# Expert-choice FFN: rows fetched and added back by indirect transfers instead of one-hot matrix products

## The chip, the cores and the metric

The kernel runs on one core of a Trainium2 chip. The metric is the device time of one execution in microseconds, lower is better. The core has TensorE (PE, matrix products; PEld is its weight load), VectorE (DVE), ScalarE (ACT), GpSimd (POOL) and SyncE (SP, which issues transfers here), and 16 DMA engines that all queues share. The queue name q0 stands for transfers that GpSimd issues, q1 for those of SyncE and ScalarE. SBUF is the on-chip memory of 128 partitions, PSUM the eight banks in which TensorE leaves results, DRAM the memory outside.

## The reference

Two transformer layers over x of 8 batches, 512 tokens and 128 channels, each with an attention and a mixture-of-experts FFN, with a modulation (scale, shift, gate per batch) around each. The change is in the FFN of the first layer, cut here to what it computes:

```python
# x: (n=8, t=512, d=128) modulated norm of the tokens; e = 8 experts; k = 2*512/8 = 128
scores = jnp.einsum('ntd,ed->nte', x, gate_w)
probs = jax.nn.softmax(scores, axis=-1)
g, m = jax.lax.top_k(probs.transpose(0, 2, 1), k)      # each expert chooses 128 tokens
xin = x[batch_idx, m]                                  # gather
h = jnp.einsum('nekd,edf->nekf', xin, w1)              # f = 512
h = jax.nn.gelu(h, approximate=False)
h = jnp.einsum('nekf,efd->nekd', h, w2)
out_tok = g[..., None] * h
out = jnp.zeros((n, t, d)).at[batch_idx, m].add(out_tok)   # scatter-add
```

The result, times the gate, is added to x; the second layer's attention reads that.

## The kernel before

The kernel is written engine by engine. One list of steps, made by `add(kind, ...)`, holds the order of the whole program; each engine walks the list and does its part of each step, waiting on semaphores. So what stands ahead in the list stands ahead in every engine's queue.

The stages, by the time at which they end in the profile: the attention of layer 0 (to 785 us) as 128 units of 5.8 us, 16 for each batch b; the FFN of layer 0 (785 to 1056 us); the attention of layer 1 as 192 units, 24 for each batch, with the second FFN's routing among them; the second FFN. In a unit of the first attention, `project` steps for the next batch make queries and keys: PE's product, ACT's copy to `raw`, two POOL products (`rope_a` L2278, `rope_b` L2280), a DVE shuffle (L1923) and a POOL sum (L2291 or L2294). `late` is one POOL product of each unit (L2330). The router's probabilities of a batch go to `prob_tok`.

The FFN works on halves of four batches and on experts x; a step r (0 to 15) is half r // 8, expert r % 8, with 4 x 128 chosen rows at once.

- **Selection** (`select`), for each half on 32 partitions (4 batches x 8 experts): 16 times the eight largest of 512 (MAX8, L1984) and their removal (MATCH_REPLACE8, L1987), then threshold, ties, running counts and slot numbers (L1989 to L2015). Half 0 is selected within the attention, half 1 during steps 0 to 5.
- **Gather**: DVE compares slot numbers with an iota into bf16 one-hot matrices (`onehots`, L2028), ACT and POOL split the tokens into three bf16 parts (`token_parts`), and PE multiplies both, 24 products of 512 columns and 32 small ones for each batch (`gather`). The gates are gathered likewise (`split_prob`).
- **Up and down**: `up0` (4 products of 512 columns, fp32), GELU on ACT, `down0` (16 products of 128 columns), and DVE's multiplication by the gate (L2045) into `y_whole`.
- **Return**: ACT and POOL split each result into three bf16 parts (`y_split`), for each batch and expert PE spreads slot numbers (`slots`, 64 products), DVE compares them (L2067), and PE adds three products into the batch's bank (`back`); DVE adds it to `xT` (L2073, semaphore `x1_ready`). `back` of batch 0 stands between the halves, that of batches 1 to 7 behind step 15 (997 to 1056 us).

During steps 8 to 15 batch 0 of the second attention is prepared: `tokens`, `stat` (two POOL instructions), `center`, `norm`, `project` of key and query, `qk_parts` (four POOL instructions each) and `copies` (four, L2304). Then SP, in this order, writes the parts (`parts_out`), the four query copies (`copy_out`), loads them (`qload`, 8), loads late tables (L1103 to L1107, after the last `down0`) and loads `q_st` and `k_st` by 12 `stack` transfers into 8 partitions each (L1132), the query's six behind `back` of half 0. The first unit of the second attention waits for them. `q_zero` is a POOL memset of `prob`.

## Time and profile before

| what | us |
| --- | --- |
| median of 3 runs | 1920.51 |
| lowest, highest | 1912.13, 1920.54 |
| span of the profiled execution | 1921.2 |
| TensorE busy in it | 1731.9 (90%) |
| VectorE, GpSimd, ScalarE busy | 1151.9, 784.0, 708.0 |
| first attention / first FFN / rest | 785.4 / 270.4 / 865.4 |

The page of the profile gives busy time by engine, the span in 40 slices, the transfers, the chain of work that ended last and the costliest groups of instructions. Its TensorE is busy in nearly every slice, so the views that tell more are the stage table (busy time between two given times), the instructions in order of time of one engine with what ended the idle time before them, and the groups by line of a stretch. The 271 us of the first FFN hold all the work that the change replaces.

### The profile page before, as it was taken

Reading aid. Unit: us, or ns where it says so; the run is one execution under the profiler, and the core shown is the slowest. Engines: PE = TensorE matmul, PEld = TensorE weight load, DVE = VectorE, ACT = ScalarE, POOL = GpSimd, SP = SyncE. Lnnn points to the kernel's source line nnn. Section 1 sums busy time; section 2 is a strip of 40 time slices with the busy share of each in tenths; the row PEclk is TensorE's granted clock in tenths of the full one; section 3 lists DMA queues with packets and bytes.
Section 4 is the critical chain, followed back from the end, with each engine's and each line's share of the span. In section 5 each row is a group of like instructions: output and inputs, shape, how many; then the busy total and the mean of one; then the engine's idle time right before and its main releaser. Section 6 shows DMA issues by size and latency. Waiting matters only on the chain.

```text
span 1921.2 us, 76644 instructions
## 1 busy us (share of the span) xinstructions
PE 1731.9 (90%) x34928; PEld 1286.5 (67%) x34928; DVE 1151.9 (60%) x2281; ACT 708.0 (37%) x1073; POOL 784.0 (41%) x760
## 2 busy tenths in 40 slices
PE   6899999999999999798999989899899898878993
PEld 4667777777777767564562767677676676668883
DVE  4656666666787875667337655666666566544324
ACT  2333444344334333342430333343333343334341
POOL 2555646564646463324250403325232343015442
PEclk9999999999999999998999999999999999989997
DMA  9600000000000000300021123131321313025666
GB/s 306 203 2 2 2 2 2 2 2 2 2 2 2 2 2 2 111 1 1 1 67 19 40 61 77 40 87 46 84 73 43 85 44 84 20 66 179 205 205 185
DMA packets 81043, 113.48 MB, mean 59 GB/s; under 512 B 9485, under 2 KB 63505, under 8 KB 80288
## 3 DMA queue, kind: packets, MB, share of 16 engines
q1 hardware_dynamic: 71376, 97.16, 18.6%
q0 software_dynamic: 4544, 8.54, 1.3%
q8 instruction: 274, 4.49, 1.0%
q10 hardware_dynamic: 4800, 2.89, 0.6%
q14 instruction: 49, 0.40, 0.1%
HBM read 83.25 MB, written 45.68 MB: 67 GB/s over the span
## 4 chain that ended last, share of the span: by engine, by line
PE 66%; DVE 18%; issue 5%; ACT 4%; DMA 4%; POOL 2%; POOLq 0%; ACTq 0%; SPq 0%; DVEq 0%
PE psum L1189 63%; DVE colmax L1935 3%; DMA arena<-in_pack 3%; ACT prob L1664 3%; DVE colmax L2092 2%; DVE ctx_sum L1947 2%; DVE raw L1923 1%; DVE rowmax L1942 1%; PE psum L1544 1%; DVE arena L2028 1%; DVE rowmax L2100 1%; PE psum L1256 1%; ACT arena L1681 1%; PE psum L1264 1%; DVE prob L1987 1%
## 5 line engine op out<-in xcount | busy, mean ns | idle before, releaser
L1189 PE MATMUL psum<-arena 128*32 128x32 f32 (+8 forms) x10552 | 576.8, 247 | 43.9 <-issue 17.2
L1189 PEld LDWEIGHTS psum<-arena 128*32 128x32 f32 (+4 forms) x10552 | 453.5, 124 | 135.1 <-issue 61.0
L1681 ACT ACTIVATE arena<-psum 128x1024 f32<-128x1024 f32 (+1 forms) x192 | 169.4, 882 | 339.8 <-PE psum L1189 339.8
L1189 PE MATMUL psum<-neg_ident,rowmax 128*32 128x128 bf16 (+3 forms) x4352 | 208.2, 248 | 10.1 <-issue 8.4
L1935 DVE TENSOR_REDUCE colmax<-psum 128x512 bf16<-128x2048 f32 (+2 forms) x96 | 168.3, 1753 | 79.4 <-PE psum L1189 79.4
L2092 DVE TENSOR_REDUCE colmax<-psum 128x256 bf16<-128x768 f32 (+2 forms) x160 | 178.2, 1114 | 59.7 <-PE psum L1189 57.3
L1189 PE MATMUL psum<-prob,ffw 128*32 128x128 f32 x5120 | 201.5, 275 | 10.9 <-DVE rowmax L1942 9.6
L1696 ACT COPY ctx_sum<-psum 128x384 f32<-128x384 f32 x128 | 61.4, 479 | 378.4 <-PE psum L1189 330.8
L2330 POOL TENSOR_TENSOR arena<-ctx_sum 128x256 f32<-128x256 f32 x128 | 94.7, 740 | 228.5 <-DVE ctx_sum L1947 216.9
L2100 DVE TENSOR_REDUCE rowmax<-psum 128x2 bf16<-128x256 f32 (+1 forms) x192 | 97.9, 510 | 145.8 <-PE psum L1189 145.7
L1664 ACT ACTIVATE prob<-psum 128x2048 f32<-128x2048 f32 (+3 forms) x128 | 158.6, 1239 | 26.3 <-PE psum L1189 25.8
L1189 PEld LDWEIGHTS psum<-neg_ident,rowmax 128*32 128x32 bf16 (+1 forms) x4352 | 135.4, 97 | 45.9 <-issue 34.1
L1189 PEld LDWEIGHTS psum<-prob,ffw 128*32 128x32 f32 x5120 | 135.9, 110 | 39.9 <-DVE rowmax L1942 26.2
L2278 POOL TENSOR_TENSOR rope_a<-raw,arena 128x512 f32<-128x512 f32 x86 | 110.9, 1289 | 120.5 <-ACT raw L1644 111.3
L1947 DVE RECIPROCAL ctx_sum<-ctx_sum 128x128 f32<-128x128 f32 x128 | 120.3, 940 | 56.5 <-ACT ctx_sum L1696 56.3
L2384 POOL DMA_INDIRECT sent<-ffw x64 | 62.6, 978 | 218.3 <-DVE ffw L2207 171.4
L1189 PEld LDWEIGHTS psum<-ident_bf,colmax 128*128 128x128 bf16 x1024 | 74.5, 98 | 98.5 <-issue 32.4
L2280 POOL TENSOR_TENSOR rope_b<-raw,arena 128x512 f32<-128x512 f32 x96 | 126.3, 1316 | 33.9 <-ACT raw L1644 26.4
L1189 PE MATMUL psum<-ident_bf,colmax 128*128 128x128 bf16 x1024 | 111.0, 221 | 30.8 <-DVE colmax L2092 20.5
L1189 PE MATMUL psum<-hT,arena 128*128 128x512 f32 (+1 forms) x276 | 129.4, 560 | 4.3 <-ACT hT L1637 2.0
L1189 PE MATMUL psum<-prob,ones_col 128*32 128x128 f32 x2560 | 128.6, 273 | 0.0
L1189 PE MATMUL psum<-prob,arena 128*32 128x32 f32 (+2 forms) x6040 | 115.0, 210 | 10.3 <-DVE ctx_sum L2045 6.5
(270 smaller groups left out, 2532.1 us busy)
## 6 DMA issues: line engine op xcount, KB each, us to landing
arena<-in_pack SPq DMA_DIRECT2D x39, 578.0 KB, 3.9
sent<-in_empty SPq DMA_DIRECT2D x9, 2112.0 KB, 35.9
arena<-qk_parts SPq DMA_DIRECT2D x96, 128.0 KB
q_copies<-arena SPq DMA_DIRECT2D x32, 256.0 KB, 3.9
prob<-q_copies SPq DMA_DIRECT2D x128, 64.0 KB, 3.5
qk_parts<-arena SPq DMA_DIRECT2D x16, 384.0 KB, 3.7
arena<-sent SPq DMA_DIRECT2D x39, 132.0 KB, 3.3
ffw<-in_L_w SPq DMA_DIRECT2D x1, 2048.0 KB, 9.3
```

The costliest lines, as they stand in the source:

```text
L1189: return pe.matmul(o, lhsT, rhs, start=start, stop=stop, skip_group_check=True)
L1664: act.activation(prob_of(u).rearrange("p z j c -> p z (j c)"), scores_of(u).rearrange("p z j c -> p z (j c)"), ACT.Exp, scale=HD0 ** -0.5) ...
L1681: act.activation(probs_of(i)[:, :, h0 * P:(h0 + nh) * P], slot(n)[:, 0:(i + 1) * W].rearrange("p (j c) -> p j c", c=W), ACT.Exp, scale=HD1 ...
L1696: act.copy(ctx_sum[:, 0, n % 2, 0:CW], psum[:, CTX, 0:CW]).then_inc(ctx_drained, 1)
L1935: dve.tensor_reduce(colmax[:, n % 2, :].rearrange("p (z c) -> p z c", z=2), scores_of(u).rearrange("p z j c -> p z c j"), AX.X, ALU.max).t ...
L1947: dve.reciprocal(ctx_sum[:, 0, n % 2, 2 * P:CW], ctx_sum[:, 0, n % 2, 2 * P:CW]).then_inc(recip, 1)
L2092: dve.tensor_reduce(colmax[:, n % 2, 0:W], slot(n)[:, 0:(i + 1) * W].rearrange("p (j c) -> p c j", c=W), AX.X, ALU.max).then_inc(colmax1_d ...
L2100: dve.tensor_reduce(rowmax[:, n % 2, 0:nh], psum[:, MAX, 0:nh * P].rearrange("p (h k) -> p h k", k=P), AX.X, ALU.max).then_inc(max_done, 1)
L2278: chain.mark(pool.tensor_tensor(rope_a[:, z, :], raw[:, z, :], table[:, 0, :], ALU.mult))
L2280: chain.mark(pool.tensor_tensor(rope_b[:, z, :], raw[:, z, :], table[:, 1, :], ALU.mult))
L2330: chain.mark(pool.tensor_tensor(ctxT[b % 2][:, 2 * q:2 * q + 2, i * P:(i + 1) * P], ctx_sum[:, 0, n % 2, 0:2 * P].rearrange("p (c q) -> p ...
L2384: pool.indirect_dma_start(sent, bass.IndirectOffsetOnAxis(ap=dest[:, b % 2, h, n:n + 1], axis=0), sent_row[:, b % 2, h, n, :], None).then_ ...
```

## The change

The selection of an expert's 128 tokens now gives gates and token numbers themselves: each of the 16 rounds adds DVE's `max_index`, and threshold, counts and slots are gone. One pair of PE transposes brings both to `slot_gate` and `slot_token`. The centred tokens of each batch are also written to DRAM (`rows_out`, SP). `fetch` is one indirect transfer for each batch and expert, issued by POOL, 128 rows of 512 bytes into `fetched`; `rows_in` is four PE transposes and four ACT copies that apply scale and shift. After `down0` the gated result lies in one of four `y_buf`, and `send_back` adds it to DRAM (`added_rows`, zeroed at the start) by one indirect accumulating transfer for each batch, each waiting for the one before of the same batch. When all eight experts of a batch have landed, SP loads the sum (`acc_in`), PE transposes it and DVE adds it to `xT` (`x1`). The `x1` of batches 0 to 3 stand in steps 8 to 13, those of 4 to 7 in the second attention (units 21, 45, 69, 93). Weights are loaded expert by expert. The tables `onehots`, `token_parts`, `split_prob`, `y_split`, `slots` and `back` are gone on all engines.

```diff
-            return ([load] + [lambda r=r: add("sel_eight", half=half, r=r) for r in range(CAP // 8)] +
-                    [lambda k=k: add(k, half=half) for k in ("sel_threshold", "sel_equal", "sel_choice", "sel_slots",
-                                                               "sel_places")] +
...
+                for k in range(2 * E):
+                    late_side.setdefault(n + NU + 10 + k, []).append(
+                        lambda k=k: fetch(k // 2, range(k % 2 * 2, k % 2 * 2 + 2)))
...
+        between = {0: [center_f], 1: [router_f]}
+        behind = {0: [norm_f], 1: choose[0:3], 2: choose[3:7], 3: choose[7:11], 4: choose[11:15],
+                  5: choose[15:] + [lambda: fetch(E, range(HALF)), lambda: fetch(E + 1, range(HALF))],
+                  6: [lambda: fetch(E + 2, range(HALF))], 7: [lambda: fetch(E + 3, range(HALF))]}
+        for r in range(E):
+            if r + 1 < E:
+                up0(r + 1)
+            for f in between.get(r, ()):
+                f()
+            add("down0", r=r)
+            if r + 2 < E:
+                rows_in(r + 2)
+            add("send_back", r=r)
+            for f in behind.get(r, ()):
+                f()
+        rows_in(E)
+        rows_in(E + 1)
+        for b in range(ABUFS):
+            acc_in(b)
+        q_zero = q_cleared()
+        between = {E: [lambda: x1(0)], E + 1: [center_a], E + 2: [lambda: begin(key_a)], E + 3: [lambda: begin(query_a)],
+                   E + 4: [lambda: x1(2)], E + 5: [lambda: turn_band(1)]}
+        behind = {E: [tokens_a, stat_a, lambda: acc_in(ABUFS)], E + 1: [lambda: add("first_place"), norm_a],
+                  E + 2: [lambda: qk_parts("key", 0), lambda: x1(1)], E + 3: [lambda: copies(0)],
+                  E + 4: [lambda: qk_parts("query", 0), lambda: turn_band(0)], E + 5: [lambda: x1(3)],
+                  E + 6: [lambda: turn_band(2)]}
...
+            if r + 2 < 2 * E:
+                rows_in(r + 2)
+            if r + 4 < 2 * E:
+                fetch(r + 4, range(HALF))
+            add("send_back", r=r)
...
+        for b in range(HALF, B):
+            at(BATCH * (b - HALF) + 21, lambda b=b: x1(b))
...
+                    elif s.kind == "acc_in":
+                        b = s["b"]
+                        w.wait_ge(d_added[b], 16 * E)
...
+                        sp.dma_start(acc[:, b % ABUFS, :, :], added_rows[b // HALF][b % HALF * S:(b % HALF + 1) * S, :].rearrange(
...
                         if b < 2:
                             w.wait_ge(y_done, 2 * E)
-                            if what == "query":
-                                w.wait_ge(backed, HALF * E)
...
+                            chain.mark(dve.max(gates[:, eight], work))
+                            chain.wait()
+                            chain.mark(dve.max_index(token[:, eight], gates[:, eight], work))
...
+                    elif k == "fetch":
...
+                            pool.indirect_dma_start(
+                                fetched[:, x, q * D:(q + 1) * D], None, token_rows[hb],
+                                bass.IndirectOffsetOnAxis(ap=slot_token[:, row:row + 1], axis=0)).then_inc(
+                                    d_fetched[x], 16)
+                    elif k == "send_back":
...
+                        w.wait_ge(y_done, r + 1)
+                        for q in range(HALF):
+                            b = hb * HALF + q
+                            w.wait_ge(d_added[b], 16 * x)
+                            pool.indirect_dma_start(
+                                added_rows[hb], bass.IndirectOffsetOnAxis(ap=slot_token[:, b * E + x:b * E + x + 1], axis=0),
+                                y_buf[:, r % YBUFS, q * D:(q + 1) * D], None, compute_op=ALU.add).then_inc(d_added[b], 16)
```

GpSimd in the first attention, from the last units of batch 6 on. Before (L2278, L2280: the two products of a projection; L2294: its sum; L2330: `late`):

```order
L2330 TENSOR_TENSOR arena<-ctx_sum 128x2x128
L2278 TENSOR_TENSOR rope_a<-raw,arena 128x512
L2280 TENSOR_TENSOR rope_b<-raw,arena 128x512
L2294 TENSOR_TENSOR ffw<-rope_a,raw 128x512
L2330 TENSOR_TENSOR arena<-ctx_sum 128x2x128
```

The same place in the changed kernel (L2149, L2151, L2165 and L2201 are those lines there, L2214 is `fetch`):

```order
L2201 TENSOR_TENSOR arena<-ctx_sum 128x2x128
L2214 DMA arena<-token_rows0,slot_token 128x128 x2
L2149 TENSOR_TENSOR rope_a<-raw,arena 128x512
L2151 TENSOR_TENSOR rope_b<-raw,arena 128x512
L2165 TENSOR_TENSOR ffw<-rope_a,raw 128x512
L2201 TENSOR_TENSOR arena<-ctx_sum 128x2x128
L2214 DMA arena<-token_rows0,slot_token 128x128 x2
```

Two indirect transfers stand between each `late` and what comes next, in 16 units, 32 in all.

GpSimd from the end of the first half on, in the changed kernel (L2226 is `send_back`, L2237 `q_zero`, L2139 and L2141 `stat`):

```order
L2226 DMA added_rows0<-arena,slot_token 2048x128 x24
L2214 DMA arena<-token_rows1,slot_token 128x128 x8
L2226 DMA added_rows0<-arena,slot_token 2048x128 x4
L2214 DMA arena<-token_rows1,slot_token 128x128 x4
L2226 DMA added_rows0<-arena,slot_token 2048x128 x4
L2214 DMA arena<-token_rows1,slot_token 128x128 x4
L2237 MEMSET prob 128x4096
L2214 DMA arena<-token_rows1,slot_token 128x128 x4
L2226 DMA added_rows1<-arena,slot_token 2048x128 x4
L2139 TENSOR_SCALAR moments<-moments 128x4
L2141 TENSOR_TENSOR rstd<-moments,minus_half 128x4
```

The eight fetches ahead of step 6's results are those of steps 8 and 9; they wait for the selection, and `stat` of the next attention stands behind a fetch and a `send_back`.

TensorE from step 5 to step 8 in the changed kernel (L1439 `rows_in`, L1429 and L1430 the transposes of the selection, L1447 `x1`, L1230 `tokens`):

```order
L1439 MATMUL psum<-ident,arena 128x128 x4
L1429 MATMUL psum<-ident,prob 128x32
L1430 MATMUL psum<-ident,prob 128x32
L1163 MATMUL psum<-arena,ffw 128x512 x4
L1163 MATMUL psum<-ffw,arena 128x128 x32
L1439 MATMUL psum<-ident,arena 128x128 x8
L1163 MATMUL psum<-arena,ffw 128x512 x8
L1447 MATMUL psum<-ident,arena 128x128 x4
L1163 MATMUL psum<-ffw,arena 128x128 x16
L1439 MATMUL psum<-ident,arena 128x128 x4
L1230 MATMUL psum<-ident,xT 128x128 x4
```

The transposes of the selection stand ahead of `up0` of step 7 and `down0` of step 6, and `x1` of batch 0 ahead of `down0` of step 8.

## Rows read from the trace of the kernel before

**Rows 1.** Stage table: stretch, its length, busy us (count) by engine, clock, DMA share, GB/s

```profile
785.40:837.20 51.80, 43.05 (x324) 25.79 (x325) 32.46 (x47) 19.01 (x32) 15.55 (x14) 0.97 0.34 103
837.20:889.80 52.60, 51.20 (x313) 38.44 (x311) 47.38 (x73) 24.65 (x46) 25.43 (x21) 1.00 0.00 1
...
935.20:996.70 61.50, 60.52 (x341) 43.34 (x342) 10.05 (x18) 29.05 (x49) 33.70 (x31) 1.00 0.12 39
996.70:1055.80 59.10, 58.85 (x224) 16.95 (x223) 44.45 (x61) 2.52 (x3) 2.43 (x3) 1.00 0.19 30
```

**Rows 2.** Order of time, TensorE in the FFN: start, us, instructions [idle before, releaser]

```profile
797.29 2.02 PE L1189 MATMUL psum<-arena 128*128 128x128 f32 x16 [3.74 <-DVE xT L1952]
...
840.79 3.60 PE L1189 MATMUL psum<-arena,ffw 128*128 128x512 f32 x8
...
847.79 3.60 PE L1189 MATMUL psum<-arena,ffw 128*128 128x512 f32 x8
...
945.76 0.60 PE L1264 MATMUL psum<-ident,ctx_sum 128*128 128x128 f32 x4
```

**Rows 3.** Groups by line and form in the FFN: busy us, mean ns

```profile
L2361 POOL TENSOR_TENSOR ctx_sum<-ctx_sum,arena 128x512 f32<-128x512 f32 x16 | 20.0, 1250 | 45.6 <-ACT arena L1745 45.2
...
L1984 DVE MAX8 prob<-prob 32x8 f32<-32x512 f32 x16 | 10.9, 680 | 0.4
L1987 DVE MATCH_REPLACE8 prob<-prob 32x512 f32<-32x512 f32 x15 | 9.9, 663 | 0.0
...
L2008 DVE TENSOR_TENSOR_SCAN prob<-prob 32x512 f32<-32x512 f32 x1 | 2.1, 2066 | 0.0
```

**Rows 4.** Stage table in pieces of 4 us around a wait of TensorE (columns of rows 1)

```profile
896.00:900.00 4.00, 3.69 (x8) 0.76 (x8) 1.66 (x3) 1.24 (x2) 2.16 (x2) 0.50 0.00 0
...
908.00:912.00 4.00, 3.06 (x15) 1.20 (x13) 0.75 (x1) 0.00 (x0) 3.08 (x1) 0.98 0.01 4
```

**Rows 5.** Indirect transfers of the second FFN: two in order of time

```profile
1216.82 0.96 POOL L2384 DMA_INDIRECT sent<-ffw  x1 [0.30 <-issue]
1218.09 0.96 POOL L2384 DMA_INDIRECT sent<-ffw  x1 [0.30 <-issue]
```

**Rows 6.** View of tensor `sent`: durations of its issues; landing times

```profile
L2384 POOL DMA_INDIRECT sent<-ffw x64: 954/958/1232, 1215.3 to 1765.7; - x64
...
DMA to landing us min/median/max: 2.2/3.2/61.1
```

**Rows 7.** View of tensor `y_rows`: landing times of 78 indirect stores and 16 loads

```profile
DMA to landing us min/median/max: 2.1/3.3/10.4
```

**Rows 8.** Order of time, GpSimd in batch 6 of the first attention

```profile
676.40 0.72 POOL L2330 TENSOR_TENSOR arena<-ctx_sum 128x256 f32<-128x256 f32 x1
...
680.73 1.27 POOL L2294 TENSOR_TENSOR ffw<-rope_a,raw 128x512 f32<-128x512 f32 x1 [0.84 <-DVE raw L1923]
682.14 0.74 POOL L2330 TENSOR_TENSOR arena<-ctx_sum 128x256 f32<-128x256 f32 x1
```

**Rows 9.** Order of time, GpSimd in the FFN

```profile
888.49 2.01 POOL L2361 TENSOR_TENSOR ctx_sum<-ctx_sum,arena 128x512 f32<-128x512 f32 x1
...
908.92 3.51 POOL L2374 MEMSET prob<- 128x4096 f32 x1 [8.77 <-PE psum L1189]
...
971.98 4.39 POOL L2304 TENSOR_TENSOR arena<-rope_a,folds 128x512 f32<-128x512 f32 x4
```

**Rows 10.** Order of time, the transfers that SyncE issues at the end of the FFN

```profile
983.79 2.54 SPq L1113 DMA_DIRECT2D q_copies<-arena  x4
989.51 3.66 SPq L1143 DMA_DIRECT2D prob<-q_copies  x8
...
999.76 25.37 SPq L1132 DMA_DIRECT2D arena<-qk_parts  x12
```

**Rows 11.** Stage table, SyncE's: stretch, length, clock, DMA share, GB/s

```profile
1004.00:1006.00 2.00, 1.00 0.55 86
...
1010.00:1011.00 1.00, 1.00 0.13 27
```

More of the change, by code:

```diff
@@ L792, in turn_band, with q_cleared @@
             band_of[k] = add("band", aux=1, k=k)
-        ahead = {E: [norm_a, lambda: begin(key_a)], E + 1: [lambda: qk_parts("key", 0)],
-                 E + 2: [lambda: begin(query_a)], E + 3: [lambda: copies(0)],
-                 E + 4: [lambda: qk_parts("query", 0), lambda: turn_band(0)], E + 5: [lambda: turn_band(1)],
-                 E + 6: [lambda: turn_band(2)]}
-        add("up0", r=E)
+        def q_cleared():
+            return add("q_zero", pool=1)
+        out0()
+        rows_in(0)
@@ L799, in build @@
+        up0(E)
         for r in range(E, 2 * E):
             if r + 1 < 2 * E:
-                add("up0", r=r + 1)
-            else:
-                for k in range(BACKS // 2):
-                    add("slots", r=E + k)
+                up0(r + 1)
+            for f in between.get(r, ()):
+                f()
             add("down0", r=r)
-            if r > E:
-                split_y(r - 1)
-            for f in ahead.get(r, ()):
+            if r + 2 < 2 * E:
[3 more added lines that the diff above has]
+            add("send_back", r=r)
+            for f in behind.get(r, ()):
@@ L822, in build @@
             stack("key", 0, r)
[L823 to L825 removed]
         for r in range(len(PARTS_Q)):
             stack("query", 0, r)
+        for b in range(HALF, HALF + ABUFS):
+            acc_in(b)
         add("v_constants", pool=2)
```

483 lines of the change are left out of this document (152 added, 331 removed).

## The prediction

> **What bounds the kernel now.** First the stage table. TensorE is busy 51.2 of 52.6 us in steps 0 to 7, 60.5 of 61.5 in steps 8 to 15 and 58.9 of 59.1 in the last return; it idles mainly around the gathers (43.1 of 51.8 in the first) [rows 1]. So the FFN, 270.4 us, is bound by TensorE, and taking products away shortens it until another queue is late. TensorE's order of time gives the price of a step (`up0` and `down0`): from 840.79 to 847.79, 7.0 us [rows 2]. Last I read GpSimd's order of time, because the change gives this queue 128 indirect transfers: it issues one each 1.27 us (1216.82 to 1218.09) [rows 5]. Four, one step's worth in one direction, are 5.1 us. I place the new FFN on the clock of the old trace and add what happens elsewhere.
>
> **Attention of layer 0: +15 us.** The 32 fetches of half 0 stand behind `late` in 16 units, 2.5 us each. In units with a projection GpSimd has no room for that: `late` at 676.40, two products, the sum at 680.73 behind a wait of 0.84 for VectorE's shuffle, the next `late` at 682.14 [rows 8], a closed loop of 5.74 us beside a unit of 5.8. VectorE's shuffle waits in order for GpSimd's product, and the column maxima for which TensorE waits stand behind the shuffle, so the delay reaches TensorE. Ten projections lie in that stretch. About five inserts fall where nothing gives way, 12.6 us; I take 13. Nothing at all (their slack covers it) and ten full inserts, 25 us, are the bounds. `max_index` adds an instruction to each of 16 rounds. It is not in this trace; next to it stand MATCH_REPLACE8, 0.66 us, and as the costliest on that shape the scan, 2.07 [rows 3]. I take 0.75 with its load, since it too passes once over 512 elements. 12 us on VectorE, less about 8 for threshold and counts: +2.
>
> **FFN, start and steps 0 to 7.** Out-projections of batch 7 cost 2.0 each, and their wait of 3.7 for VectorE behind the one-hots goes [rows 2]; `up0` of step 0 can start at 797.0. Its weights, the first 0.5 MB of 4, have 11 us by then; the zeros and the tokens' copy in DRAM are written long before anyone reads them, and ScalarE, busy 24.7 of 52.6 us [rows 1], trades two casts a step for four small copies: 0 for each. Eight steps are 56.2, six `rows_in` of 0.45 (four transposes; the row of 0.60 holds the end of the last one) [rows 2] 2.7, norm, router and transposes 2.5, a wait for the norm 1.0. The selection decides more. A round is now 0.68 + 0.75 + 0.75, with gaps 2.2 us [rows 3], 35.5 for 16. It starts at 819.5, lets four gate multiplications (0.7 each) in, loses 2 us to order, and ends at 859.8. TensorE, whose transposes of it stand ahead of `up0` of step 7, is there at 848.9: a wait of 11.0, which the old selection, shorter by the indices, did not cause. Such a wait costs twice: TensorE's clock was 0.50 of full (1.2 GHz) in 896 to 900, after it had stood idle since 889.8, and 0.98 again in 908 to 912 [rows 4]; with half of the work at half speed I add 4. Half 0 ends at 874.4.
>
> **FFN, steps 8 to 15.** GpSimd can fetch half 1 from 861.5. Ahead of the last `send_back` of batch 0 it issues 17 transfers (8 fetches, 4 sends, 4 fetches, 1 send), 21.5 us, to 883.0. Landing 3.2 [rows 6], SP's issue 0.5 and the load about 3 give 889.7; TensorE has been there since 883 and waits 6.7 for `x1` of batch 0. Then `stat` stands behind two groups of four and the memset of 3.5 [rows 9], and the norm comes 6.2 late; the query's projection leaves its bank 4.7 late, because ACT's copy waits for `qk_parts` of the key. With 54 us of TensorE's own work from 893.7 step 15 ends at 958.6. GpSimd: from 883.0 three sends 3.8, four fetches 5.1, memset 3.5, then until the query's parts nine groups of four 45.5, `stat`, key and query work 13.2, `copies` 4.4 [rows 9], and the query's parts 3.7: 962.2. It is later than TensorE, so it sets the end.
>
> **The handover.** SP writes the parts (0.4), the copies 2.54, waits 3.2 for them, loads 3.66 [rows 10], tables 2.3: 974.4. Then 12 stacks stand in a row. Before, the first six were issued from 999.8 and the transfers had fallen to a share of 0.13 at 1010 to 1011 [rows 10, 11], 10 us; the other six hid under `back`. Both now lie open: 20.3. The second attention begins at 994.7, after some 36 us of an idle TensorE, instead of 1055.8. That is **-61.1**.
>
> With six in flight the share was 0.55 at 86 GB/s [rows 11]. The Trainium skill ("DMA: Bandwidth & Descriptors", "Why a DMA increments its semaphore by 16 and not by 1") has a transfer use as many engines as divide its outermost dimension, here 8 of 16, and the lowest ones; the trace agrees, and by it 12 take twice as long as 6. Without such a limit twelve at once could share the idle half and end 10 us earlier, at 1872 in all.
>
> **Attention of layer 1: +7 us.** Four `x1`, with 0.5 us of TensorE and 0.75 of VectorE each, some of it hidden: 3. The lower clock after the long wait: 4 [rows 4]. Everything later is unchanged. If the return's transfers of half 1 land late, nobody asks before unit 21.
>
> **Sum:** 1921.2 + 15 - 61.1 + 7 = **1882 us**. The profiled execution's span, 1921.2, and the median, 1920.5, are so near that I use the figure for both.
>
> **Rivals.**
> - *The fetches of half 0 hide, GpSimd is still late in the FFN.* For: VectorE loses the old threshold steps just there. Against: the loop of rows 8. 1882 - 15 = 1867.
> - *GpSimd is never late.* Then the query's parts, on which the end hangs, would be made at 941, TensorE's own pace, 21 us earlier. With the hidden fetches 1882 - 21 - 15 = 1846. Against: the count of transfers; it would need issues well under 1.27.
> - *Slower than before: accumulating transfers land late.* `send_back` of a step waits for the landing of the last step's for the same batch, and the whole GpSimd queue with it. No row shows one; plain indirect ones land after 3.2 and 3.3, the latest of `y_rows` after 10.4 [rows 6, 7]. I take 3.2 since all are 128 rows of a similar size. A step is 7.45 with its transposes, so up to about 6 us it costs nothing. At 13 half 0 takes 14.3 a step, 48 more on seven steps less the 15 around the selection, and half 1 adds 4.2 on five: +54, 1936. It passes the old time from about 12 on.
> - *Everything at its dear end*: ten full inserts (+12), the index at 1.4 (+10), GpSimd's chain late by 15 more: 1919, no change. That is also the case in which the removed products turn out to have been only a cover for the stacks.
> - *Contention at each issue.* GpSimd's product at 888.49 beside VectorE's one-hots took 2.01, where the mean of its line is 1.25 [rows 3, 9]. If each of some 60 transfers on the chain had those 0.76, and 15 in the attention: 1882 + 46 + 11 = 1939. Against it: 64 issues lie between 954 and 1232 ns [rows 6], with VectorE busy more than half of the time.
>
> The Trainium skill ("SBUF: State Buffer", box "The DVE blocks DMA trap (SWDGE)") says that VectorE in a two-port mode keeps GpSimd from writing descriptors. It would give the last rival; the narrow spread of the 64 issues speaks against it here.
>
> **How the numbers follow.** Forecast 0.52 (own range 1862 to 1906), hidden fetches 0.18, GpSimd never late 0.08, late landings 0.12, no change 0.05, contention 0.05. A measurement of this kernel can tell about 0.5%, 10 us, from no change. Faster by more than that, under 1911: 0.52 + 0.18 + 0.08 = 0.78. Within: the no-change case and an edge of the late landings, 0.07. Slower 0.15. The range from 1844 to 1914 takes in the first three and leaves out the slower ones.
>
> **What would show it.** In the changed kernel's profile: batch 6 and 7 of the first attention some 13 us longer, with VectorE's shuffle waiting for GpSimd; FIND_INDEX near 0.7 us; TensorE idle about 11 us before the selection's transposes and 7 before the first `x1`; accumulating transfers landing after 3 to 4 us; GpSimd past 60% busy from step 5 to 15; the first scores of the second attention some 209 us after the first attention's end, behind the last stack. I am wrong if the first attention keeps its length, if TensorE idles at `send_back`'s expense in half 0, or if the stacks land in under 15 us.

## The result and the profile after

The changed kernel takes 1906.3 us (median of 14 runs, 1893.9 to 1914.4), the kernel before 1918.9 in the same session: a ratio of 0.993, 95% interval 0.991 to 0.995. It is faster by 13 us, where 39 were forecast. The profiled execution's span is 1907.4 us.

The stage table of the changed kernel, with the columns of [rows 1]: half 0 up to step 3, steps 3 to 5, the selection and the first `x1`, steps 9 to 15, and the handover to the second attention.

```profile
811.50:849.10 37.60, 31.28 (x188) 24.39 (x188) 8.62 (x29) 17.86 (x37) 9.83 (x9) 0.95 0.56 153
849.10:877.10 28.00, 23.04 (x132) 16.69 (x133) 23.69 (x57) 12.93 (x25) 18.60 (x13) 1.00 0.32 29
877.10:935.20 58.10, 40.36 (x203) 28.60 (x203) 15.69 (x42) 18.23 (x37) 45.66 (x37) 0.88 0.35 57
935.20:1013.20 78.00, 54.61 (x308) 39.48 (x306) 11.45 (x23) 22.62 (x44) 65.22 (x53) 0.85 0.26 39
1013.20:1042.60 29.40, 0.00 (x0) 0.01 (x1) 0.69 (x1) 0.00 (x0) 20.74 (x13) 0.55 0.85 161
```

TensorE, busy almost throughout in [rows 1], is busy 149.3 of the 231.1 us, and GpSimd is the fullest engine from 877 on (110.9 of 136.1 up to 1013). TensorE's granted clock is 0.85 in the fourth row, where it waits often. The first attention now ends at 811.5 instead of 785.4, the FFN takes 231.1 instead of 270.4, and the rest 864.8 instead of 865.4: +26.1, -39.3 and -0.6, together -13.8, the difference of the two spans.

**First attention.** Two rows of each kernel, ScalarE's first and last exponential: in the kernel before 739.86 us lie between them, in the changed one 763.39, so 23.5 of the 26 arise inside. The other 2.5 lie ahead of the first exponential; kernels with the same start had it at 40.5 to 44.4, so they are not the change's.

```profile
41.26 1.88 ACT L1664 ACTIVATE prob<-psum 128x2048 f32<-128x2048 f32 x1 [7.46 <-PE psum L1189]
781.12 0.60 ACT L1664 ACTIVATE prob<-psum 128x512 f32<-128x512 f32 x1
```

```profile
43.75 1.88 ACT L1606 ACTIVATE prob<-psum 128x2048 f32<-128x2048 f32 x1 [9.04 <-PE psum L1163]
807.14 0.60 ACT L1606 ACTIVATE prob<-psum 128x512 f32<-128x512 f32 x1
```

GpSimd in order of time where a fetch pair meets a projection; it answers to [rows 8].

```profile
682.60 0.73 POOL L2201 TENSOR_TENSOR arena<-ctx_sum 128x256 f32<-128x256 f32 x1
683.48 0.99 POOL L2214 DMA_INDIRECT arena<-token_rows,slot_token  x1
684.77 0.94 POOL L2214 DMA_INDIRECT arena<-token_rows,slot_token  x1 [0.31 <-issue]
685.74 1.27 POOL L2149 TENSOR_TENSOR rope_a<-raw,arena 128x512 f32<-128x512 f32 x1
687.08 1.26 POOL L2151 TENSOR_TENSOR rope_b<-raw,arena 128x512 f32<-128x512 f32 x1
689.19 1.26 POOL L2165 TENSOR_TENSOR ffw<-rope_a,raw 128x512 f32<-128x512 f32 x1 [0.84 <-DVE raw L1841]
690.59 0.73 POOL L2201 TENSOR_TENSOR arena<-ctx_sum 128x256 f32<-128x256 f32 x1
```

The loop from one `late` to the next is 7.99 us instead of 5.74. The waits of VectorE in 672 to 811 show who pays (waiting instruction, releaser, us in total, times, longest):

```profile
DVE raw L1841 <- POOL rope_b L2151: 38.6, 9, 5.3
```

Before, this wait was 10.7 us, 6 times. The loops from one `late` to the next that hold a fetch pair, the same 16 in both traces, in us:

| loops with a fetch pair | count | before | changed | longer |
| --- | --- | --- | --- | --- |
| a projection's products behind the pair | 9 | 57.4 | 73.4 | 16.0 |
| no projection | 7 | 35.6 | 40.8 | 5.2 |

Five of the nine are 2.2 to 2.4 us longer, nearly all of a pair's 2.5; the other four, longer before (6.5 to 7.2 us), grow by 0.8 to 1.5. Together that is 21.2 of the 23.5 us; the rest was there ahead of the first pair.

**FFN.** The transfers by group (first row of the page, second of the stretch 811 to 1045) and the landing of the accumulating ones; they answer to [rows 5, 6].

```profile
L2226 POOL DMA_INDIRECT added_rows<-arena,slot_token x64 | 100.0, 1563 | 33.7 <-issue 16.8
...
L2214 POOL DMA_INDIRECT arena<-token_rows,slot_token x32 | 31.4, 982 | 10.1 <-issue 8.7 <-DVE raw L1841 1.0 <-DVE moments L1817 0.3
```

```profile
DMA to landing us min/median/max: 3.2/3.3/8.8
```

A fetch is a plain indirect transfer and costs what was forecast, 0.98 us and one each 1.27. An accumulating one takes 1.56 us, and with the 0.30 of issue between them one each 1.86.

TensorE's longest waits in the FFN, in order of time; they answer to [rows 2].

```profile
814.71 3.58 PE L1163 MATMUL psum<-arena 128*128 128x128 f32 x16 [3.36 <-POOLq L1021]
888.98 0.24 PE L1429 MATMUL psum<-ident,prob 32*128 32x32 f32 x1 [4.18 <-DVE prob L1910]
922.10 1.12 PE L1447 MATMUL psum<-ident,arena 128*128 128x128 f32 x4 [10.46 <-DMA arena<-added_rows]
946.30 1.12 PE L1238 MATMUL psum<-ident,ctx_sum 128*128 128x128 f32 x4 [7.83 <-DVE ctx_sum L1826]
980.07 6.24 PE L1163 MATMUL psum<-arena,ffw 128*128 128x512 f32 x8 [11.65 <-ACT arena L1657]
1042.62 0.59 PE L1163 MATMUL psum<-causal,ident_bf 128*128 128x512 bf16 x1 [29.46 <-DMA arena<-qk_parts]
```

A step of half 0, TensorE: `up0`, `down0`, `rows_in`, and again `up0`.

```profile
849.15 3.67 PE L1163 MATMUL psum<-arena,ffw 128*128 128x512 f32 x8 [1.21 <-issue]
852.65 3.73 PE L1163 MATMUL psum<-ffw,arena 128*128 128x128 f32 x32
856.23 0.60 PE L1439 MATMUL psum<-ident,arena 128*128 128x128 f32 x4
858.47 3.67 PE L1163 MATMUL psum<-arena,ffw 128*128 128x512 f32 x8 [1.64 <-issue]
```

It is 9.32 us, not 7.45: `up0` stands right behind its own transposes and waits for ScalarE's four copies of them. The profile calls that wait "issue"; the experiment with the rows ahead shows what it is.

The end of the query's parts on GpSimd, and SyncE's transfers after it, which answer to [rows 10]:

```profile
1010.23 1.16 POOL L2193 TENSOR_TENSOR arena<-ctx_sum,arena 128x512 bf16<-128x512 f32 x1
```

```profile
1011.79 2.52 SPq L1089 DMA_DIRECT2D q_copies<-arena  x4
1018.69 3.69 SPq L1117 DMA_DIRECT2D prob<-q_copies  x8
...
1025.25 6.91 SPq L1106 DMA_DIRECT2D arena<-qk_parts  x12
```

### The profile page after: what moved, and what is told of

Read it like the earlier page. It is cut to its first block, busy times and chain, and to the rows that moved or that the text cites. A ratio compares the mean times of both kernels' runs of the same rounds, so it can differ in the third digit from the quotient of the medians.

```text
span 1907.4 us, 75393 instructions
## 1 busy us (share of the span) xinstructions
PE 1648.4 (86%) x34316; PEld 1268.5 (67%) x34316; DVE 1054.0 (55%) x2219; ACT 695.3 (36%) x1071; POOL 880.8 (46%) x836
## 4 chain that ended last, share of the span: by engine, by line
PE 59%; DVE 16%; POOL 8%; issue 7%; DMA 5%; ACT 4%; SPq 1%; POOLq 0%; ACTq 0%; DVEq 0%
PE psum L1163 56%; DVE colmax L1853 3%; DMA arena<-in_pack 3%; POOL added_rows L2226 3%; ACT prob L1606 2%; DVE colmax L1963 2%; POOL arena L2214 2%; DVE ctx_sum L1865 2%; DVE raw L1841 1%; DVE rowmax L1860 1%; PE psum L1486 1%; POOL rope_a L2149 1%; POOL rope_b L2151 1%; DVE rowmax L1971 1%; PE psum L1238 1%
## 5 line engine op out<-in xcount | busy, mean ns | idle before, releaser
L1163 PEld LDWEIGHTS psum<-arena 128*32 128x32 f32 (+3 forms) x10296 | 448.5, 126 | 132.3 <-issue 59.2
L1163 PE MATMUL psum<-prob,ffw 128*32 128x128 f32 x5120 | 204.9, 278 | 23.5 <-DVE rowmax L1860 22.0
L1853 DVE TENSOR_REDUCE colmax<-psum 128x512 bf16<-128x2048 f32 (+2 forms) x96 | 168.4, 1754 | 77.5 <-PE psum L1163 77.5
L2201 POOL TENSOR_TENSOR arena<-ctx_sum 128x256 f32<-128x256 f32 x128 | 94.2, 736 | 221.6 <-DVE ctx_sum L1865 210.0
L1606 ACT ACTIVATE prob<-psum 128x2048 f32<-128x2048 f32 (+3 forms) x128 | 158.6, 1239 | 30.3 <-PE psum L1163 29.7
L2149 POOL TENSOR_TENSOR rope_a<-raw,arena 128x512 f32<-128x512 f32 x86 | 110.7, 1287 | 94.9 <-ACT raw L1586 86.6
L2151 POOL TENSOR_TENSOR rope_b<-raw,arena 128x512 f32<-128x512 f32 x96 | 125.4, 1307 | 36.6 <-ACT raw L1586 29.2
L1163 PE MATMUL psum<-causal,ident_bf 128*128 128x256 bf16 (+1 forms) x448 | 111.9, 297 | 35.1 <-DMA arena<-qk_parts 29.5
L2226 POOL DMA_INDIRECT added_rows<-arena,slot_token x64 | 100.0, 1563 | 33.7 <-issue 16.8
```

The source lines that it names most:

```text
L1163: return pe.matmul(o, lhsT, rhs, start=start, stop=stop, skip_group_check=True)
L1606: act.activation(prob_of(u).rearrange("p z j c -> p z (j c)"), scores_of(u).rearrange("p z j c -> p z (j c)"), ACT.Exp, scale=HD0 ** -0.5) ...
L1853: dve.tensor_reduce(colmax[:, n % 2, :].rearrange("p (z c) -> p z c", z=2), scores_of(u).rearrange("p z j c -> p z c j"), AX.X, ALU.max).t ...
L2149: chain.mark(pool.tensor_tensor(rope_a[:, z, :], raw[:, z, :], table[:, 0, :], ALU.mult))
L2151: chain.mark(pool.tensor_tensor(rope_b[:, z, :], raw[:, z, :], table[:, 1, :], ALU.mult))
L2201: chain.mark(pool.tensor_tensor(ctxT[b % 2][:, 2 * q:2 * q + 2, i * P:(i + 1) * P], ctx_sum[:, 0, n % 2, 0:2 * P].rearrange("p (c q) -> p ...
```

## The experiments

Each is the changed kernel with one or more edits. Two lengths are read from each trace. The **lag** is the time from ScalarE's first exponential to its last in the first attention, less 739.9, that of the kernel before. The **FFN stretch** goes from the first product of batch 7's output projection behind the barrier to the first scores of the second attention.

The first twelve runs were on three chips on which the kernel before takes 1988 to 1996 us. There the whole surplus lies in the second attention and what follows (the changed kernel: 944.8 us behind the first scores instead of 864.8, at a granted clock of 0.90 in 1300 to 1400 instead of 0.97), while both lengths above are the same within 2.2 us. The last three runs (e13 to e15) were on a chip on which the kernel before takes 1917.3, as on the first. So ratios are to the kernel before on the same chip, and the two lengths are compared directly. The changed kernel itself was not run on the chip of the last three.

| kernel | ratio, 95% interval | lag | FFN stretch |
| --- | --- | --- | --- |
| changed kernel (first chip) | 0.993 (0.991 to 0.995) | 23.5 | 227.9 |
| e5 changed kernel again | 0.995 (0.993 to 0.997) | 22.0 | 230.1 |
| e1 bursts of four | 0.997 (0.995 to 0.999) | 23.7 | 228.5 |
| e6 half 0 by SyncE, no choice | 0.981 (0.979 to 0.983) | 0.3 | 230.0 |
| e9 half 0 plain by GpSimd, no choice | 0.984 (0.981 to 0.987) | 5.6 | 230.1 |
| e7 pairs, two experts in the FFN | 0.988 (0.985 to 0.990) | 11.2 | 234.0 |
| e2 rows ahead | 0.995 (0.992 to 0.997) | 22.4 | 225.2 |
| e3 scatter without adding | 0.989 (0.985 to 0.992) | 22.0 | 214.3 |
| e4 parts first | 0.992 (0.989 to 0.995) | 22.0 | 220.8 |
| e8 pairs, rows, parts, tables | 0.989 (0.985 to 0.992) | 11.3 | 223.8 |
| e10 e8 without rows ahead | 0.989 (0.986 to 0.992) | 11.7 | 227.2 |
| e11 e8, selection's transposes later | 0.987 (0.984 to 0.991) | 11.7 | 225.5 |
| e12 e11 without parts first | 0.989 (0.987 to 0.992) | 11.7 | 234.6 |
| e13 fetches where GpSimd idles | 0.981 (0.977 to 0.984) | 3.0 | 232.0 |
| e14 e13 with rows, parts, tables | 0.980 (0.977 to 0.983) | 2.9 | 218.1 |
| e15 e14 without rows ahead | 0.983 (0.980 to 0.985) | 3.0 | 223.9 |

### What made the first attention longer

**e5**, the reference on such a chip: 

> The changed kernel unchanged, for a ratio taken on the chip of the experiments beside it: 0.993 of the kernel before, as on the first chip. If the second attention depends on the chip and not on the change, its length differs from 865 us by the same in every run of this chip.

Measured 0.995. What lies behind the first scores is 933 to 955 us long in all twelve runs of these chips, whatever the edit, so the surplus belongs to the chip, as written.

**e1**, half 0's fetches in eight bursts of four:

```diff
-                for k in range(2 * E):
-                    late_side.setdefault(n + NU + 10 + k, []).append(
-                        lambda k=k: fetch(k // 2, range(k % 2 * 2, k % 2 * 2 + 2)))
+                for k, at in enumerate((15, 20, 23, 24, 25, 26, 27, 28)):
+                    late_side.setdefault(n + NU + at, []).append(lambda k=k: fetch(k, range(HALF)))
```

> The changed kernel with one thing moved: the 32 fetches of half 0 stand in eight units of the first attention's last stretch without a projection (four batches at once, one expert each) instead of two at a time in 16 units in a row. Theory (inserts into GpSimd's loop with VectorE made the first attention longer by 21 us): the lag of batches 6 and 7 goes, the last context of attention 0 leaves 15 to 21 us earlier than the changed kernel's 811.5, nothing later changes, 1906 becomes 1886 to 1891. Rival (the added max_index and the selection on VectorE made it longer): the first attention keeps its length within 4 us and the time is 1902 to 1910. Rival 3 (eight bursts of 5 us each are as bad as 16 of 2.5): 1900 to 1910 with the lag now in batch 7 alone.

The theory's number failed and the third rival came true: until unit 120, with three bursts, the lag was 6.9 instead of 20.5, then it grew by 17 in the last seven units, with five. Four in a row, 5 us, nearly fill a unit of 5.8 by themselves.

**e6**, half 0's rows by SyncE:

```diff
+                    elif s.kind == "fetch" and s["r"] < E:
...
+                        for q in s["batches"]:
+                            sp.dma_start(fetched[:, x, q * D:(q + 1) * D], token_rows[0][q * S:q * S + P, :]).then_inc(
+                                d_direct, 16)
```

> The changed kernel, but half 0's rows come by 32 plain transfers that SyncE issues at the same places; it leaves out the choice in half 0 (the first 128 tokens of each batch are taken). max_index, the selection's waits, all landings and the sends stay. Theory (GpSimd's 32 issues made the first attention longer by 23 us, the index and the traffic almost nothing): the last context of attention 0 leaves 20 to 23 us earlier than the changed kernel's, all later lengths stay, 18 to 23 us under the changed kernel. Rival (max_index on VectorE, busy 70% there): 12 us or less of it goes. Rival (the rows' packets in the DMA engines hold up others): under 5 us goes.

The lag is 0.3, and the time (1954.6) 26 us under e5's 1981.1, 3 more than expected. So `max_index` costs the first attention nothing at its end (the lag is 2.8 at unit 106 and is made up again), plain transfers of the same size issued by SyncE cost nothing, and all of the lag goes with the indirect transfers on GpSimd's queue.

```profile
40.91 1.88 ACT L1614 ACTIVATE prob<-psum 128x2048 f32<-128x2048 f32 x1 [7.46 <-PE psum L1171]
781.05 0.60 ACT L1614 ACTIVATE prob<-psum 128x512 f32<-128x512 f32 x1
```

**e9**, the same plain transfers from GpSimd's queue:

```diff
+                        for q in s["batches"] if hb == 0 else ():
+                            pool.dma_start(fetched[:, x, q * D:(q + 1) * D], token_rows[0][q * S:q * S + P, :]).then_inc(
+                                d_fetched[x], 16)
```

> The changed kernel with half 0's 32 fetches as plain transfers, issued from GpSimd's queue at the same places; it leaves out the choice in half 0 (the first 128 tokens of each batch are taken). It tells what of the 22 us that the first attention lost is GpSimd's time and what is the kind of transfer. Theory (each transfer that GpSimd issues costs its queue about 1.25 us, whatever kind): the lag stays at 15 to 23 us. Rival (only an indirect one costs that, since each partition's index is read): issues under 0.5 us, lag under 5. In both cases: if TensorE's groups of products break up with idle time of kind 'issue' behind these too, the cause is how GpSimd's transfers are queued; if they do not, it is the indices.

Both numbers lie between theory and rival. From the view of `token_rows`, plain ahead of indirect:

```profile
L2213 POOL DMA_DIRECT2D arena<-token_rows x32: 544/577/793, 673.0 to 763.4; - x32
L2217 POOL DMA_INDIRECT arena<-token_rows,slot_token x32: 943/948/1404, 873.1 to 967.9; - x32
```

0.58 us with no gap behind it instead of 1.27, and a lag of 5.6 instead of 22. The lag follows GpSimd's time, not in proportion: 18 us of issuing made 5.6, 40 made 22 to 23.5. That the first part fits into slack is argued, not shown, since the kind of transfer changed too.

**e7**, 24 fetches in pairs in 12 units chosen as free of a projection, the last eight in the FFN:

```diff
+                for k, at in enumerate((12, 15, 16, 20, 23, 24, 25, 26, 27, 28, 29, 30)):
+                    late_side.setdefault(n + NU + at, []).append(
+                        lambda k=k: fetch(k // 2, range(k % 2 * 2, k % 2 * 2 + 2)))
...
+        behind = {0: [norm_f, lambda: fetch(E - 2, range(HALF))], 1: [lambda: fetch(E - 1, range(HALF))] + choose[0:3],
```

> The changed kernel with half 0's fetches in pairs in 12 of attention 0's units where GpSimd has no projection (24 of them), and the last eight behind steps 0 and 1 of the FFN. Theory of slack (GpSimd has 4.9 us of a 5.8 us unit free there, a pair takes 2.5, so nothing gives way): attention 0's lag falls from 23.5 to under 6 us, and the FFN stays within 2 us; 14 to 19 under the changed kernel. Rival (in the run with bursts of four the lag came in free units too, 3.3 us each, so a fetch holds up the others even where GpSimd has room): the lag stays at 12 or more, and the time within 8 us of the changed kernel.

Between the two cases: the lag is 11.2, and 13 us come off (1968.2). The FFN stretch is 3.9 longer than in e5, not within 2. Three of the 12 pairs stand directly ahead of a projection's products in GpSimd's queue after all, and these three loops are 6.3 us longer than in the kernel before. But half of the lag arises in units 120 to 127, where GpSimd itself waits 2.1 to 3.4 us in each unit. TensorE's groups break up there. In e7, while a pair's rows move:

```profile
761.06 0.59 PE L1163 MATMUL psum<-prob,ffw 128*32 128x128 f32 x6
761.93 0.44 PE L1163 MATMUL psum<-prob,ffw 128*32 128x128 f32 x6 [0.29 <-issue]
762.66 0.32 PE L1163 MATMUL psum<-prob,ffw 128*32 128x128 f32 x2 [0.29 <-issue]
```

From 672 to 783 us TensorE waits 2.9 us in this way ("issue") in e7 and 2.3 us in e5, but not at all in e9, whose plain transfers stand where e5 has its indirect ones. In the changed kernel's own trace and in e13 there is no such row either, and six of e13's pairs leave their loops as long as before, where e7's in the same six loops cost up to 1.4 us each. So it was seen with indirect transfers on the three slower chips only, and what connects the two is not settled here.

### What set the pace of the FFN

**e3**, the scatter without adding:

```diff
-                                y_buf[:, r % YBUFS, q * D:(q + 1) * D], None, compute_op=ALU.add).then_inc(d_added[b], 16)
+                                y_buf[:, r % YBUFS, q * D:(q + 1) * D], None).then_inc(d_added[b], 16)
```

> The changed kernel with the scatter plain instead of accumulating: it leaves out the adding, so that in a token's row the last expert's output stays. All 64 transfers, waits and landings stay. Theory (an accumulating transfer costs GpSimd 1.86 us an issue where a plain one costs 1.26, and GpSimd's queue sets x1 of batch 0 and the query's parts): 0.6 us less on each; about 8 stand ahead of the last send of batch 0 from the selection's end on, and 28 more until the query's parts: the second attention starts up to 17 us earlier, 1889 to 1896. Rival (TensorE's own steps set the end, GpSimd only looks late): under 4 us, 1902 to 1908. Second rival (accumulating and plain issue cost the same, the price is from the registers of this line): L2226 still shows about 1.56 us busy and 1.86 a period.

```profile
L2226 POOL DMA_INDIRECT added_rows<-arena,slot_token x64: 956/967/1108, 835.2 to 1008.8; - x64
```

The theory holds: 0.97 us instead of 1.56, and the FFN stretch is 15.8 shorter than in e5. The time goes just where the sends stand: from the selection's transposes to `x1` 29.7 us instead of 33.0, from `x1` to the query's parts 76.5 instead of 89.6, while the handover is 0.5 longer. In these two parts GpSimd issues 28 sends, and 28 times 0.59 us are 16.5. That is the price of "accumulating" on GpSimd's queue.

**e2**, the fetched rows' transposes ahead of `down0`:

```diff
-            add("down0", r=r)
             if r + 2 < E:
                 rows_in(r + 2)
+            add("down0", r=r)
```

> The changed kernel with the transposes of the fetched rows (rows_in of step r+2) put ahead of down0 of step r instead of behind it. Theory (up0 of the step after stands right behind its own rows and waits 1.65 us a step for ScalarE's four copies): the steps of half 0 fall from 9.3 to 7.6 us, seven of them, and half 1 gains 1.2 on up to six where GpSimd is not the bound: 12 to 19 us off, 1887 to 1894. Rival (the queue of GpSimd with its transfers sets the pace, TensorE's wait for copies is only where the slack shows): half 0 shortens, but the wait for the selection and for x1 of batch 0 grows by the same, 1900 to 1907.

The rival: steps fall to 7.44 us, as the rows show (`up0` to `up0`), and TensorE's wait for the selection grows from 4.2 to 9.6. Of some 13 us, about 5 reach the end (225.2 against 230.1, and nothing that the ratio shows). Five such steps stand ahead of the selection's transposes, 9.4 us: 5.4 of them go into the wait, and the selection itself ends 4.0 earlier.

```profile
849.34 3.60 PE L1163 MATMUL psum<-arena,ffw 128*128 128x512 f32 x8
852.77 0.60 PE L1439 MATMUL psum<-ident,arena 128*128 128x128 f32 x4
853.21 3.74 PE L1163 MATMUL psum<-ffw,arena 128*128 128x128 f32 x32
856.78 3.60 PE L1163 MATMUL psum<-arena,ffw 128*128 128x512 f32 x8
...
881.41 0.31 PE L1429 MATMUL psum<-ident,prob 32*128 32x32 f32 x1 [9.58 <-DVE prob L1910]
```

**e4**, GpSimd's other work of a step ahead of its transfers in steps 8 to 15:

```diff
...
+            for f in behind.get(r, ()):
+                f()
             if r + 4 < 2 * E:
                 fetch(r + 4, range(HALF))
             add("send_back", r=r)
-            for f in behind.get(r, ()):
-                f()
```

> The changed kernel with GpSimd's order inside steps 8 to 15 changed: tokens, statistics, norm, the memset, the parts of key and query and the copies stand ahead of that step's fetch and send_back instead of behind them. Theory (the second attention starts where the query's parts are made, and these stand behind transfers for which nobody waits yet): the parts come 7 to 20 us earlier, and 1906 becomes 1888 to 1899. Rival (x1 of batch 0 at 922 binds everything behind it, the transfers behind it only fill): 1902 to 1908. Rival on the other side (the sends come later, so that x1 of batches 1 and 2 and the fetches of steps 12 to 15 come late): TensorE idles in steps 12 to 15 and the time is 1910 or more.

The theory holds: the FFN stretch is 9.3 shorter than in e5. The query's parts are ready 190.0 us behind the stretch's start instead of 197.4, without a transfer less.

**e8**, all of these with e7's fetches, the table loads behind the stacks: 

> The changed kernel with the fetches of the run named before, the rows' transposes ahead of down0, GpSimd's parts ahead of its transfers in steps 8 to 15, and the five table loads behind the twelve stacks. If these are independent terms: attention 15, steps 3, parts 7, tables 2 to 3, about 27 us under the changed kernel, a ratio of 0.980 to the kernel before. If GpSimd's queue binds behind all of them, the terms don't add: 12 to 18 under it, 0.985.

1966.0 us, 15 under e5 on the same chip, and a ratio of 0.989: the second case, the terms do not add. Attention gave 11, but the FFN only 6 against e5, less than e4 alone. The selection's transposes come 1.9 earlier than in e5, but from there to `x1` it takes 36.4 us instead of 33.0.

**e10**, e8 without rows ahead: 

> The changed kernel with pairs of fetches in units without a projection, GpSimd's parts ahead of its transfers in steps 8 to 15, and the table loads behind the stacks; rows_in stands behind down0 as in the changed kernel. Theory (rows ahead of down0 only moves the wait to the selection, so leaving it out costs nothing): attention 11, FFN 7 to 11, together 18 to 22 under the changed kernel, ratio 0.984 to 0.986. Rival (the fetches of steps 6 and 7 behind steps 0 and 1 delay the sends until the selection ends): the FFN gains under 5.

Its rival: 227.2, 6 more than e4. Only 2.5 of these lie ahead of the selection's transposes, where the fetches behind steps 0 and 1 can delay the sends; 3.9 lie in the handover, and why is not shown.

**e11**, the selection's transposes behind `down0` of step 6:

```diff
+            if r == E - 2:
+                choose[17]()
+                fetch(E, range(HALF))
+                fetch(E + 1, range(HALF))
             add("send_back", r=r)
```

> The kernel with all four reorderings and one more: the selection's transposes stand behind down0 of step 6 on TensorE, ahead of that step's send_back on GpSimd, instead of behind step 5. Theory (TensorE, with the rows ahead of down0, reaches the selection 10.6 us early and could work a step meanwhile): that wait goes to 0 to 3, the step that it used to do afterwards is done, half 0 ends 7 to 10 us earlier; of that 3 to 8 reach the second attention, since fetch and send_back still stand in GpSimd's queue. Ratio 0.981 to 0.985. Rival (GpSimd's queue from the selection's end on sets everything): x1 of batch 0 is at the same time, 0.987 to 0.989 as with four reorderings.

TensorE's wait for the selection falls from 10.6 to 4.3, and then it waits 7.0 and 3.9 for the fetched rows; `x1` of batch 0 starts at 909.86 against 909.91 in e8. The rival holds: from the selection on, GpSimd's queue sets the time.

**e12**, e11 with the parts behind the transfers again: 

> As the run before, but with GpSimd's transfers ahead of its parts in steps 8 to 15, as in the changed kernel. Where the parts bind (as they did alone, 9 us of FFN): 7 to 10 us slower than the run before. Where x1 and the sends bind: within 3 us of it.

The stretch is 9.1 longer, as expected, but the medians differ by only 2.3 us, and the ratios (0.989 and 0.987) do not tell the two apart.

### Is it the transfers, or where they stand?

**e13**, only the fetches moved: 16 in pairs in eight units chosen as free of a projection, 12 right behind the barrier, four behind `stat`:

```diff
+                for k, at in enumerate((16, 20, 23, 24, 25, 26, 27, 28)):
+                    late_side.setdefault(n + NU + at, []).append(
+                        lambda k=k: fetch(k // 2, range(k % 2 * 2, k % 2 * 2 + 2)))
...
         out3()
+        for r in range(4, 7):
+            fetch(r, range(HALF))
         up0(0)
         tokens_f()
         stat_f()
+        fetch(7, range(HALF))
```

> The changed kernel with only the fetches of half 0 moved: those of experts 0 to 3 in eight pairs in units without a projection, those of 4 to 6 right behind the barrier, where GpSimd idles 16.1 us in the changed kernel (12 by 1.26 are 15.1), those of 7 behind the statistics of batch 7. Theory (the cost of a fetch is where it stands): attention 0's lag is 4 to 8 us instead of 22, the FFN within 2 us of 229, 13 to 18 under the changed kernel. Rival (fetches moved into the FFN delay it, as the two experts' behind steps 0 and 1 did by 4 to 6): FFN 233 or more, 8 to 12 under.

1884.4 us, a ratio of 0.981 where the changed kernel had 0.993: by the ratios some 20 us under it on this chip. The lag is 3.0, less than expected. Six of the eight pairs cost nothing (each of their loops is as long as in the kernel before, within 0.01 us); the other two stand directly ahead of a projection's products, and their loops are 1.8 and 2.2 us longer. GpSimd behind the barrier, first and last of 12 fetches and `stat`:

```profile
792.19 1.10 POOL L2217 DMA_INDIRECT arena<-token_rows,slot_token  x1 [0.16 <-issue]
...
806.12 0.94 POOL L2217 DMA_INDIRECT arena<-token_rows,slot_token  x1 [0.30 <-DVE moments L1820]
807.10 0.25 POOL L2142 TENSOR_SCALAR moments<-moments 128x4 f32<-128x4 f32 x1
```

So the queue had room for nearly all 32; the attention's 22 us were a matter of place. The FFN stretch is 2 to 4 longer, not within 2 of 229. It is the handover: TensorE's wait is 34.8 us instead of 29.5, since the twelve stacks take 22.8 instead of 17.4, although the query's parts come no later (195.5 us behind the stretch's start). Why was not traced.

**e14**, with e8's other three edits: 

> As the run before, with rows ahead of down0, GpSimd's parts ahead of its transfers in steps 8 to 15, and the table loads behind the stacks. Theory (terms add where each has idle time of its own): attention 14 to 18, FFN 216 to 219 instead of 229 (parts 9, rows 3): 25 to 30 under the changed kernel, ratio 0.979 to 0.982 to the kernel before. Rival (they meet in GpSimd's queue): FFN 222 or more, ratio 0.984 or more.

The FFN is 218.1, as the theory has it, and 13.9 under e13. The ratio is in the theory's range too, and by it the kernel is some 24 us under the changed one. But the total, 1880.8 (ratio 0.980), is only 3.6 under e13, within the intervals: what lies behind the first scores is 868.4 us instead of 862.0, of which 3.3 arise in its first 75 us, at a clock of 0.93 instead of 0.96. The rest was not traced further. Its ratio is the lowest of all, clear of the changed kernel's, but not told apart from e13's and e15's.

**e15**, e14 without rows ahead: 

> As the run before, but rows_in behind down0 as in the changed kernel. If the rows' place is worth 3 us here too: FFN 219 to 222 and 3 slower than the run before. If TensorE just waits longer for the selection: the same as the run before within 1.5.

223.9, 5.8 longer than e14 and more than expected: here the rows' place has a part of its own. 4.5 of it lie ahead of the selection's transposes, and from there to `x1` both take 33.2 us, unlike e8. In time it is 2.8 us, within the intervals.

## Why the prediction was right or wrong

The sign and the mechanism were right, the size was not: 13 to 14 us instead of 39. The measured 1906.3 lies at the upper edge of the forecast's own range (1862 to 1906) and inside the wide one (1844 to 1914). Two steps failed. The larger one is the price of a `send_back` on GpSimd's queue: the forecast took 1.27 us for every transfer, and an accumulating one measured 1.86. The other is the term for the inserts, 13 us, where the loops with a fetch pair became 21.2 us longer. Term by term:

- **Start and attention, +15 forecast, +26.1 measured.** 2.5 of it is the start. The mis-sized term is the 13 us for "about five inserts where nothing gives way". The loop of rows 8 was read rightly, and five projection loops did pay in full, 11.4 us. But the others were put at nothing: four projection loops paid 4.6 us in part, and the loops without a projection 5.2. (Nine projections meet a fetch pair, not ten.) The bound of ten full inserts, 25 us, was nearer the truth. TensorE's granted clock also fell, to 0.87 in 700 to 740, where it had been 1.00; but in e5 it was 1.00 from 672 to 803 and the lag still 22.0, so the clock hardly explains more than the 1.5 us between the two.
- **`max_index`, +2 forecast.** An instruction takes 0.67 us and its load 0.08, as forecast; in the attention it alone costs nothing (e6: lag 0.3). The 16 of half 1:

```profile
L1904 DVE FIND_INDEX8 prob<-prob 32x8 uint32<-32x512 f32 x16 | 10.8, 673 | 0.0
```

- **FFN to the selection's end, 74.4 us forecast, 77.5 measured** (from the attention's end). Two errors hid each other, which is luck. The step is 9.3 us and not 7.45, since ScalarE's copies had been taken to cost nothing, so TensorE arrives 9.8 us later than forecast; the wait for the selection is 4.2 and not 11. e2 shows how they are linked: 9.4 us less of steps lengthen the wait by 5.4 and move the selection's end by 4.0.
- **To `x1` of batch 0, 29.9 forecast, 33.1 measured** (888.98 to 922.10). The 12 fetches and 5 sends take 24.2 us and not 21.5: five sends at 1.86 are 3 more. The landing was 3.3, as assumed.
- **From `x1` to the query's parts, 72.5 forecast, 89.3 measured.** This is the largest error. The count was right: behind the last send of batch 0 (from 917.4 to 1011.4) GpSimd issues 23 sends and 20 fetches, the 43 that were counted. The price was not: I took 1.27, the period of plain indirect transfers [rows 5], for both kinds. 23 sends at 1.86 are 13.6 more. The trace had no accumulating transfer, and I bounded only when one lands, not what one costs to issue. The 28 sends of this part and the one before account for 16.5 of the 21.8 us by which the FFN was forecast too short, and e3, which takes only the adding away, gives 16.4 back in just these two parts.
- **Handover, 32.5 forecast, 31.2 measured.** The twelve stacks, 20.3 forecast, took 17.4 from the first issue to the first scores, and 17.1 to 25.0 in the other runs. The DMA share was 0.77 to 0.98 in three pieces of 2 us, with sends and sums of batches 4 to 6 among them, so this stretch bears out neither limit by itself. The forecast had followed the Trainium skill's rule on how many engines a transfer uses ("DMA: Bandwidth & Descriptors", "Why a DMA increments its semaphore by 16 and not by 1"); its 20.3 lies within the measured spread.
- **Second attention, +7 forecast, -0.6 measured.** Four `x1` and the lower clock after the handover leave no trace in its length. Whether something else gained what they cost, no run shows.
- **Rivals.** Late landings: refuted, 3.3 us median and 8.8 at most, and GpSimd waited 0.6 us in all for them. Contention at each issue: refuted, 64 fetches between 940 and 1405 ns with a median of 950, half of them beside a VectorE that is busy 49% of 700 to 740, the others beside one busy 15 to 27%. The Trainium skill warns of a trap ("SBUF: State Buffer", box "The DVE blocks DMA trap (SWDGE)"): while VectorE runs in a two-port mode, GpSimd cannot write descriptors. It does not show in these durations; whether VectorE ever ran in such a mode here, the trace does not say. Hidden fetches: refuted for this order, and almost true for another (e13).

From -61.1 to -39.3 in the FFN, and from +15 to +26.1 ahead of it, less the 7.6 that the second attention did not cost: 22 + 11 - 8 = 25 us, the distance from 1882 to 1907.

## What to carry to other kernels

An indirect transfer is work for GpSimd, and its price is GpSimd's time at the place where it stands: count the issues, each kind at its own price, and put them where that engine idles. Thirty-two of them cost 22 us in a row of units most of which hold a projection; moved elsewhere they cost 3 there and 2 to 4 us in the FFN. In a closed loop of two engines a turn without slack pays in full, and a turn with some still pays a part: read the slack of each turn, and look in the queue itself at what stands behind the inserted work.

## What the runs showed of the hardware

- On GpSimd's queue a plain transfer of 128 rows of 512 bytes takes 0.58 us (e9), a plain indirect one 0.95 to 0.98 and 1.27 a period, an accumulating indirect one 1.56 and 1.86 a period. Dropping only the addition brings 1.56 down to 0.97 (e3).
- FIND_INDEX8 on 32 partitions of 512 elements: 0.67 us, as the other two passes of a round.
- The same program took 1906 us on one chip and 1981 on another. Both first attentions and FFNs have the same length within 3 us; the second attention was 80 us longer at a lower granted clock.
- On the three slower chips TensorE's groups of small products broke up, with idle time of kind "issue" (4.0 us in e10 from 672 to 793, none in e9 with plain transfers), while indirectly fetched rows moved. Not seen on the faster chips, and not explained.
